# Attention over the input itself in a deep local-attention layer, with value and output weights multiplied beforehand, and expert mixing by gating the input

## The chip, the cores and the metric

The kernel runs on one core of one Trainium2 chip. The metric is the time of one execution on the device in microseconds (us), median over several runs. TensorE (PE) multiplies, VectorE (DVE), ScalarE (ACT) and GpSimd (POOL) work on elements, and SyncE (SP) starts the DMAs. Each engine takes its own instructions strictly in the order in which they are written; between engines there are counting semaphores and nothing else.

## The reference, cut to what matters

Twelve residual sublayers run over x of 4 units x 512 positions x 128 features, all in float32. The change touches three of their parts. The deep sublayer (called twice) is by far the longest:

```
for i in range(6):                                # DEPTH
    s = shift_tokens(x)
    q, k, v = split(s @ Wqkv[i])                  # 16 heads of 64
    q, k = l2norm(q) * qs, l2norm(k) * ks; rotary(q), rotary(k)
    attn = softmax(8 * q @ k2.T, masked)          # windows of 32 queries over 64 keys
    x = (attn @ v2) @ Wo[i] + x
    x = layernorm(shift_tokens(x)) -> gated gelu (341 hidden) -> + x
```

The mixture (called twice) is `gate = softmax(x @ Wg + bg)`, the top 2 of 8 experts kept and normalised, and `out = sum over e of gate[e] * (x @ We[e].T + be[e])`. Ahead of each of the twelve sublayers stands a plain layer norm.

## The kernel before, in words

Activations lie features by positions: 128 features on the partitions, 512 positions of a unit along the free axis. Four units (b = 0 to 3) go through each sublayer.

**Deep stage.** A call has 6 layers x 4 units = 24 units (`UNITS`) of 4 tiles of 128 positions, so 96 tiles. The order is written out by hand as a software pipeline: one step s handles tile s in its projection, tile s-1 in its norm and rotation's end, tile s-2 in its scores and softmax, and tile s-3 in the product of probabilities and values. n = s // 4 is the unit, t = s % 4 the place in it. Each engine has a loop over s (`deep_pe`, `deep_act`, `deep_dve`, `deep_pool`) that names its pieces in a fixed order, with extra pieces of the unit's end (output projection, layer norm, gated gelu) at particular t. On PE a step of the kernel before is:

1. `qk_pe(s, 0)`, L1307: queries, 2 matmuls of 512 columns. Here the step begins (called T0 below).
2. `scores_open_pe`, L1262 and L1276; `value_pe`, L1332 (4 matmuls of 64 x 512, two heads' halves in different columns of the array); `scores_close_pe`, L1276.
3. the unit's pieces of this t (t=0 variance, t=1 gate 0, t=2 hidden 2, t=3 rest of Wo).
4. `turn_pe(s-1, 0)`, L1320: 8 transposes of the rotated queries. It waits for POOL's `rope_scale_pool(s-1, 0)`, L1739, which waits for ACT's square root `norms_act(s-1)`, L1487. On ACT that stands behind `square_act(s, 0)`, L1480, which waits for piece 1.
5. `qk_pe(s, 1)` for the keys; `mix_open_pe(s-3)`, L1359 (probabilities x values, 32 small matmuls of 64 x 64 x 32 columns); `turn_pe(s-1, 1)`; `mix_close_pe`; `probs_turn_pe(s-2)`, L1290; and among them further pieces of the unit's end.

PE computes a float32 matmul as two passes, so 2 matmuls of 512 columns are 4 entries in the trace; a transpose (`is_transpose=True`) is one. The values of a window lie once in each half of the partitions; `value_act` evacuates half of them and four DMAs of SP (`move_values`) copy the rest.

**Mixture.** For each of 16 tiles of 128 positions PE forms all 8 experts' outputs (L375, 2 matmuls of 512 columns), DVE multiplies them by the gates (L473, 1024 elements) and adds over experts (L478), PE transposes the sum back (L400), and after four tiles DVE adds it to x (L463). One unit has four tiles.

**Layer norm ahead of a sublayer.** `quad_spread_pe`, L184, spreads 1/std over the partitions: 16 matmuls with the identity for four units, in two passes each; DVE's L206 scales with it.

Of the kernel before, what the change touches and what calls it, by code (L numbers as in the profile page):

```python
# [39 lines left out]
ODD_LAYER = 34430  # L40
# [5 lines left out]
def program(nc, d, out, sublayers):  # L46
    with ExitStack() as ctx:
# [19 lines left out]
        layered = [n for n in d if n.startswith("deep_")]  # L67
# [35 lines left out]

        kept = {n: sb("w_" + n, list(d[n].shape), d[n].dtype) for n in lasting}
# [72 lines left out]
        def quad_spread_pe(pe, q, b):  # L177
# [18 lines left out]
        def quad_centre_dve(dve, q, at_=small):  # L196
            for b in range(NB):
                dve.wait_ge(qn.qn_mean_ready, NB * q + b + 1)
                nc.vector.tensor_tensor(at_.xc[:, b, :], x[:, unit(b)], norm_bank(b), ALU.subtract).then_inc(qn.qn_centred, 1)
            dve.wait_ge(qn.qn_std_ready, q + 1)  # L200
            nc.vector.reciprocal(all_rstd[:, :], all_std[:, :]).then_inc(qn.qn_rstd_ready, 1)
# [125 lines left out]
        def swiglu_dve(dve, u, q, k):  # L327
# [3 lines left out]
            for b in range(NB):  # L331
# [5 lines left out]
                if b >= 1:  # L337
# [4 lines left out]
        mo = sems("moe_logits_ready moe_step moe_shifted moe_exped moe_gsum moe_ginv moe_gates_ready moe_gates_turned moe_gates_kept "  # L342
                  "moe_experts_ready moe_weighted moe_summed moe_out_ready")
# [26 lines left out]
        def moe_experts_pe(pe, k, i):  # L370
            b, t, a = i // TILES, i % TILES, 2 * (i % 2)
            if i >= 2:
                pe.wait_ge(mo.moe_weighted, TILES * k + i - 1)
            for h in range(2):
                last = nc.tensor.matmul(bank(a + h), qn_xn[:, b, 1 + t * P:1 + (t + 1) * P], w.moe_we[:, 4 * h:4 * h + 4, :],  # L375
                                        start=True, stop=True)
            last.then_inc(mo.moe_experts_ready, 1)

        def moe_gates_pe(pe, k, b):
# [5 lines left out]
            for t in range(TILES):  # L385
                last = nc.tensor.matmul(norm_bank(b)[0:EXPERTS, t * P:(t + 1) * P], gates[:, TILES * b + t, :], w.ident[:, :],
                                        start=True, stop=True)
            last.then_inc(mo.moe_gates_turned, 1)

        def moe_bias_pe(pe, u, k, b):  # L390
            if b >= 1:
                pe.wait_ge(g.unit_done, u + b)
            pe.wait_ge(mo.moe_gates_kept, k + b + 1)
            nc.tensor.matmul(bank(4), w.moe_be[:, :], gatesT[0:EXPERTS, b, :], start=True, stop=False, skip_group_check=True)

        def moe_turn_pe(pe, k, i):

            t = i % TILES
            pe.wait_ge(mo.moe_summed, TILES * k + i + 1)
            last = nc.tensor.matmul(bank(4)[:, t * P:(t + 1) * P], moe_acc[:, i % 2, :], w.ident[:, :],  # L400
                                    start=False, stop=(t == TILES - 1), skip_group_check=True)
            last.then_inc(mo.moe_out_ready, 1)

        def moe_pe(pe, u, q, k):
# [17 lines left out]
        def moe_act(act, q, k):
# [3 lines left out]
            for b in range(NB):  # L426
                act.wait_ge(mo.moe_gates_turned, k + b + 1)
                nc.scalar.activation(gatesT[0:EXPERTS, b, :], norm_bank(b)[0:EXPERTS, :], ACT.Copy).then_inc(mo.moe_gates_kept, 1)

        def moe_route_dve(dve, r):  # L430
# [27 lines left out]
            nc.vector.tensor_tensor(gates, ex, over(ginv, G), ALU.mult).then_inc(mo.moe_gates_ready, 1)  # L458
            dve.wait_ge(mo.moe_gates_ready, r + 1)

        def moe_out_dve(dve, k, b):
            dve.wait_ge(mo.moe_out_ready, TILES * (k + b + 1))
            nc.vector.scalar_tensor_tensor(x[:, unit(b)], bank(4), 0.5, x[:, unit(b)], ALU.mult, ALU.add).then_inc(g.unit_done, 1)  # L463

        def moe_dve(dve, u, q, k):
            quad_centre_dve(dve, q)
# [3 lines left out]
            for i in range(ROWS):  # L470
                a, n = 2 * (i % 2), TILES * k + i
                dve.wait_ge(mo.moe_experts_ready, n + 1)
                nc.vector.tensor_tensor(moe_prod[i % 2], psum[:, a * 512:(a + 2) * 512].rearrange("p (e o) -> p e o", o=P),  # L473
                                        over(gates[:, i, :], [P, EXPERTS, P]), ALU.mult).then_inc(mo.moe_weighted, 1)
                dve.wait_ge(mo.moe_weighted, n + 1)
                if i >= 2:
                    dve.wait_ge(mo.moe_out_ready, n - 1)
                nc.vector.tensor_reduce(moe_acc[:, i % 2, :], moe_prod[i % 2].rearrange("p e o -> p o e"), AX.X,  # L478
# [1618 lines left out]
```

## Time and profile before

| | us |
|---|---|
| median of 3 runs | 4492.48 (4480.17 to 4496.16) |
| profiled execution, its own time | 4489.61 |
| its span | 4487.9 |
| deep calls, about 1060 to 2720 and 2820 to 4488 of the span | some 3300 |
| mixtures, 11 to 94.4 and 373 to 456 | some 165 |

One execution was profiled. A matmul's end in the trace is modelled, so the time from the start of one group of matmuls to the start of the next is what PE spent on it. "128*64" in a row is the part of the array used (rows*columns), 128x512 the output. Idle time in square brackets names who ended it.

### The profile page before, as it was taken

What the parts mean: (1) busy time and instruction counts of PE and PEld (TensorE: products, weight loads), DVE (VectorE), ACT (ScalarE), POOL (GpSimd) and SP (SyncE); (2) the same over time, 40 slices, a digit from 0 to 9 for tenths busy, and PEclk for the clock granted to TensorE, in tenths of its full rate; (3) what the DMA queues carried; (4) which work ended last, traced back from release to release, by engine and by line L of the source; (5) the groups of instructions that cost most, each with busy time, mean ns of one, the idle gap of its engine ahead of it and who ended that gap; (6) DMA issues with size and microseconds to landing.
All of it is one profiled execution on the core that took longest, in us unless ns stands there. A gap on an engine that the chain in (4) does not pass through costs nothing.

```text
span 4487.9 us, 148433 instructions
## 1 busy us (share of the span) xinstructions
PE 4237.0 (94%) x66604; PEld 2403.9 (54%) x66604; DVE 3256.5 (73%) x4169; ACT 2676.0 (60%) x3161; POOL 2128.2 (47%) x1151
## 2 busy tenths in 40 slices
PE   7998899867999999999999996799999999999998
PEld 4544433434555555555555553455555555555554
DVE  6566666565877877877877866677877877877874
ACT  1451355323776776776776762466766766766764
POOL 0110000013665665666665650566666666666663
PEclk8998899978999999999999997899999999999999
DMA  2000000001111211121121111111211211121111
GB/s 84 1 2 1 0 1 1 1 0 35 33 33 29 58 33 54 33 58 30 33 58 29 33 33 50 24 31 31 58 32 31 58 32 55 33 57 30 33 33 29
DMA packets 78612, 144.88 MB, mean 32 GB/s; under 512 B 18648, under 2 KB 24992, under 8 KB 76448
## 3 DMA queue, kind: packets, MB, share of 16 engines
q1 hardware_dynamic: 77984, 135.39, 11.7%
q8 instruction: 530, 8.68, 0.8%
q14 instruction: 98, 0.80, 0.1%
HBM read 39.91 MB, written 1.05 MB: 9 GB/s over the span
## 4 chain that ended last, share of the span: by engine, by line
PE 77%; POOL 8%; issue 7%; DVE 6%; ACT 2%; DMA 0%; SPq 0%; POOLq 0%; DVEq 0%; ACTq 0%
PE psum L1307 13%; PE psum L1359 7%; PE psum L1332 6%; PE psum L1320 6%; PE psum L1276 5%; PE psum L667 5%; PE psum L1378 5%; PE psum L1290 4%; POOL arena L1739 3%; PE psum L1408 3%; PE psum L1424 3%; PE psum L1418 3%; PE psum L1373 3%; PE psum L699 3%; PE psum L721 3%
## 5 line engine op out<-in xcount | busy, mean ns | idle before, releaser
L1739 POOL TENSOR_TENSOR arena<-arena 128x1024 f32<-128x1024 f32 x384 | 722.3, 1902 | 881.8 <-ACT arena L1487 881.8
L1733 POOL TENSOR_TENSOR arena<-arena 128x1024 f32<-128x1024 f32 x384 | 907.5, 2363 | 245.0 <-DVE arena L1608 245.0
L1604 DVE TENSOR_TENSOR arena<-psum,arena 128x1024 f32<-128x1024 f32 x384 | 467.6, 1218 | 616.8 <-ACT arena L1480 616.6
L1480 ACT ACTIVATE arena<-psum 128x1024 f32<-128x1024 f32 x384 | 392.4, 1022 | 288.2 <-PE psum L1307 288.2
L1359 PEld LDWEIGHTS psum<-arena 64*64 64x64 f32 x24576 | 395.6, 135 | 211.8 <-issue 211.8
L1493 ACT ACTIVATE arena<-psum 128x1024 f32<-128x1024 f32 x384 | 390.8, 1018 | 194.6 <-PE psum L1320 194.6
L1608 DVE TENSOR_TENSOR arena<-psum,arena 128x1024 f32<-128x1024 f32 x384 | 466.4, 1215 | 0.0
L1615 DVE TENSOR_REDUCE h_pair<-arena 128x16 f32<-128x1024 f32 x384 | 464.2, 1209 | 0.0
L1359 PE MATMUL psum<-arena 64*64 64x32 f32 x24576 | 437.9, 221 | 5.2 <-DVE arena L1582 5.1
L1320 PE MATMUL psum<-w_ident,arena 128*128 128x128 f32 x3072 | 416.3, 279 | 23.5 <-POOL arena L1739 15.1
L1320 PEld LDWEIGHTS psum<-w_ident,arena 128*128 128x128 f32 x3072 | 338.2, 141 | 162.0 <-POOL arena L1739 94.6
L1307 PE MATMUL psum<-deep_wqkv,arena 128*128 128x512 f32 x768 | 378.6, 617 | 26.3 <-DVE arena L1608 19.3
L1745 POOL TENSOR_TENSOR arena<-arena 128x1024 f32<-128x1024 f32 x192 | 365.3, 1903 | 66.9 <-DVE arena L1592 58.4
L1276 PEld LDWEIGHTS psum<-arena 64*32 64x32 f32 x24576 | 292.9, 105 | 167.9 <-issue 157.8
L1307 PE MATMUL psum<-arena 128*128 128x512 f32 x768 | 361.9, 592 | 0.0
L1504 ACT ACTIVATE arena<-psum 128x1024 f32<-128x1024 f32 x192 | 196.7, 1024 | 257.9 <-PE psum L1290 251.6
L1276 PE MATMUL psum<-arena 64*32 64x64 f32 x24576 | 327.2, 223 | 0.3 <-issue 0.2
L667 PE MATMUL psum<-arena 32*128 32x512 f32 (+3 forms) x1024 | 303.6, 590 | 3.4 <-ACT arena L806 2.3
L1497 ACT ACTIVATE arena<-arena 128x1024 f32<-128x1024 f32 x192 | 202.9, 1057 | 173.8 <-DVE arena L1582 173.8
L699 PE MATMUL psum<-arena 32*128 32x512 f32 (+3 forms) x1024 | 293.3, 558 | 1.8 <-ACT arena L831 1.8
L1575 DVE TENSOR_REDUCE arena<-psum 128x16 f32<-128x1024 f32 x192 | 235.2, 1225 | 61.1 <-PE psum L1276 61.1
L831 ACT ACTIVATE arena<-psum 128x512 f32<-128x512 f32 (+3 forms) x344 | 161.0, 514 | 170.8 <-PE psum L699 169.4
(266 smaller groups left out, 7087.0 us busy)
## 6 DMA issues: line engine op xcount, KB each, us to landing
arena<-arena SPq DMA_DIRECT2D x672, 128.0 KB, 2.4
deep_wqkv<-in_deep_wqkv SPq DMA_DIRECT2D x6, 1536.0 KB, 7.2
arena<-in_deep_wqkv SPq DMA_DIRECT2D x6, 1536.0 KB, 7.1
arena<-arena SPq DMA_DIRECT2D x96, 64.0 KB, 2.0
deep_wo<-in_deep_wo SPq DMA_DIRECT2D x6, 512.0 KB, 7.5
arena<-in_deep_wo SPq DMA_DIRECT2D x6, 512.0 KB, 7.5
deep_w<-in_deep_w SPq DMA_DIRECT2D x6, 341.0 KB, 7.6
arena<-in_deep_w SPq DMA_DIRECT2D x6, 341.0 KB, 7.6
```

What stands on the lines that cost most here:

```text
L667: nc.tensor.matmul(bank(v % SCORE_BANKS)[:, 0:keys], da_Q[r32, b * SETS + s, x_ * P:(x_ + 1) * P], keys_of(causal, b, s)[r32, 0:keys], sta ...
L699: nc.tensor.matmul(bank(key_at[m])[:, q0:T], kk[r32, kt * P:(kt + 1) * P], da_Q[r32, b * SETS + s, q0:T], start=True, stop=True).then_inc( ...
L1276: last = nc.tensor.matmul(bank(r)[32 * jj:32 * jj + 32, pair * 64:pair * 64 + 64], qT[j % 2][r64, pair, jj * WIN:(jj + 1) * WIN], kT[r64, ...
L1307: last = nc.tensor.matmul(bank(2 + cc), xs[unit_ % 2][:, WIN + t * P:WIN + (t + 1) * P], wqkv[:, half * INNER + cc * 512:half * INNER + (c ...
L1320: last = nc.tensor.matmul(turns[:, m * P:(m + 1) * P], roped[a % 2][:, h:h + 2, :], w.ident[:, :], start=True, stop=True, is_transpose=True)
L1359: last = nc.tensor.matmul(bank(odd)[64 * side:64 * side + 64, to:to + WIN], V[64 * r:64 * r + 64, WPT * t + jj, (pair + odd) * 64:(pair + ...
L1480: nc.scalar.activation(qk_sq[:, HALVES[half], :], qk_half, ACT.Square).then_inc(de.deep_qk_squared, 1)
L1604: nc.vector.tensor_tensor(turned[:, hs, :].rearrange("p h (a e) -> p h a e", a=2), swapped, sin, ALU.mult).then_inc(de.deep_rope_parts, 1)
L1608: nc.vector.tensor_tensor(roped[a % 2][:, hs, :], qk_half, under(tabs[:, 2 * half, t, :], shape), ALU.mult).then_inc(de.deep_rope_parts, 1)
L1615: nc.vector.tensor_reduce(h_pair[:, hs, 0], qk_sq[:, hs, :], AX.X, ALU.add).then_inc(de.deep_sq_summed, 1)
L1733: nc.gpsimd.tensor_tensor(roped[a % 2][:, hs, :], roped[a % 2][:, hs, :], turned[:, hs, :], ALU.add).then_inc(de.deep_summed, 1)
L1739: nc.gpsimd.tensor_tensor(roped[a % 2][:, hs, :], roped[a % 2][:, hs, :], over(h_inv[a % 2][:, hs], [P, LHEADS, LD]), ALU.mult).then_inc(d ...
```

## The change

**Deep attention.** Instead of values V = X Wv and then P V Wo, the kernel forms P X (probabilities of a head times the input of the 64 keys, 128 features wide), and multiplies that by Wv_h Wo_h, a 128 x 128 matrix for each of the 16 heads.

- `value_pe` and `value_act` go. `xt_pe` (2 transposes) and `xt_act` (256 elements) put the transposed input of the tile's windows into `XA`; two DMAs (`move_keys`) make `XB`, the same with halves exchanged.
- `mix_pe` has 4 matmuls of 64 x 128 x 256 columns in each of its two parts instead of 32 of 64 x 64 x 32. Each part now fills both banks 0 and 1, so part 1 waits until ACT's `o_act(part 0)` has emptied them; ACT copies 1024 elements per part (`Y`), twice a tile instead of once.
- `out_pe` replaces `wo_first_pe` and `wo_rest_pe`: per unit 2 halves x 16 heads of 256 columns instead of 8 matmuls of 512 columns.
- `fold_pe` computes Wv_h Wo_h: 4 matmuls of 128 columns a unit for 20 of the 24 units (the next layer's), and 16 ahead of each call, between the layer norm's statistics and its spread. `fold_act` copies them.
- The unit's end moves by one tile or more: mean at the end of t=0, variance at t=1, gate 0, 1 and 2 at t=2, a 0 and 1 at t=3, a 2 and down at t=0 of the following unit. Gate, gelu and a use bank 7 alone, so gate 1 waits for gelu 0 and gate 2 for gelu 1.

**Mixture.** `moe_spread_pe` spreads the gates of four experts over the partitions (4 matmuls of 32 x 128 x 512 columns side by side), DVE multiplies the input by them (4 x 512 elements), and `moe_expert_pe` adds up 8 matmuls of 512 columns and one of the bias per unit in PSUM. Two rounds of four experts a unit, 8 rounds in all.

**Layer norm.** `quad_spread_pe` gets `is_transpose=True`: one pass instead of two.

```diff
-        def value_pe(pe, c, a):
...
-            for q in range(2):
-                wi = WPT * t + 2 * q + 1
                 for r in range(2):
-                    last = nc.tensor.matmul(turns[64 * r:64 * r + 64, q * 512:(q + 1) * 512],
-                                            xs[unit_ % 2][:, WIN * wi:WIN * wi + 2 * WIN], vw[:, r, :, :], start=True, stop=True)
+        def xt_pe(pe, c, a):
...
+            for n in range(2):
+                at = WIN * (WPT * t + n)
+                last = nc.tensor.matmul(turns[:, n * P:(n + 1) * P], xs[unit_ % 2][:, at:at + P], w.ident[:, :], start=True, stop=True,
+                                        is_transpose=True)
+        def mix_pe(pe, c, j, part):
+            if part == 0:
...
+            else:
+                pe.wait_ge(de.deep_o_kept, 2 * i + 1)
+            for side in range(2):
+                for r in range(2):
+                    r64, jj = slice(64 * r, 64 * r + 64), 2 * part + side
+                    keys = (XA if r == part else XB)[j % 2]
+                    last = nc.tensor.matmul(bank(r)[:, side * 256:(side + 1) * 256], keys[r64, side, :], weights[r64, :, jj, :],
+                                            start=True, stop=True)
+        def fold_pe(pe, c, layer, k, to):
+            for n in range(FOLD_HEADS):
+                pair, r64 = FOLD_HEADS * (k // 2) + n, slice(64 * (k % 2), 64 * (k % 2) + 64)
+                last = nc.tensor.matmul(to[:, n * P:(n + 1) * P], unfolded["deep_wvt"][r64, pair, :], unfolded["deep_wo"][r64, pair, :],
+                                        start=True, stop=True)
+        def out_pe(pe, c, m, half, part):
...
+            for h in range(8 * part, 8 * part + 8):
+                at = (h % 2) * 256 + (h // 2) * WIN
+                last = nc.tensor.matmul(bank(6)[:, half * 256:half * 256 + 256], vo[:, h, :], Y[half][:, :, at:at + WIN],
+                                        start=(h == 0), stop=(h == LHEADS - 1))
         def gate_pe(pe, c, m, j):
...
-                pe.wait_ge(de.deep_gelu_done, 3 * g_ + 1)
+                pe.wait_ge(de.deep_gelu_done, 3 * g_ + j)
+                if t == 1 and 1 <= n <= FOLDED_UNITS:
+                    fold_next_pe(pe, c, n)
+                if t == 0 and ending:
+                    out_pe(pe, c, n - 2, 1, 1)
+                if t >= 1 and begun:
+                    out_pe(pe, c, n - 1, (t - 1) // 2, (t - 1) % 2)
                 if 0 <= s - 3 < ALL:
-                    mix_close_pe(pe, c, s - 3)
+                    mix_pe(pe, c, s - 3, 1)
```

On PE, a step of a full unit with t=2 in the kernel before, from T0 on (L1307 projection, L1332 values, L1418 hidden 2, L1320 the turn of queries and then keys, L1359 mix, L1424 down, L1373 Wo):

```order
L1307 MATMUL psum<-deep_wqkv,arena 128x512 x2
L1262 MATMUL psum<-maskb,identb 32x512 x8
L1276 MATMUL psum<-arena 32x64 x32
L1332 MATMUL psum<-deep_wqkv,arena 64x512 x4
L1276 MATMUL psum<-arena 32x64 x32
L1418 MATMUL psum<-xc,deep_w_0 85x512
L1320 MATMUL psum<-w_ident,arena 128x128 x8
L1307 MATMUL psum<-deep_wqkv,arena 128x512 x2
L1359 MATMUL psum<-arena 64x32 x32
```

The same step in the changed kernel (L1326 projection, L1349 `xt_pe`, L1438 gate, L1339 turn, L1368 mix, L1403 `out_pe`):

```order
L1326 MATMUL psum<-arena 128x512 x2
L1279 MATMUL psum<-maskb,identb 32x512 x8
L1293 MATMUL psum<-arena 32x64 x32
L1349 MATMUL psum<-w_ident,arena 128x128 x2
L1293 MATMUL psum<-arena 32x64 x32
L1438 MATMUL psum<-xc,deep_w_0 128x512
L1339 MATMUL psum<-w_ident,arena 128x128 x8
L1326 MATMUL psum<-arena 128x512 x2
L1368 MATMUL psum<-arena 128x256 x4
L1339 MATMUL psum<-w_ident,arena 128x128 x8
L1438 MATMUL psum<-xc,deep_w_0 128x512
L1403 MATMUL psum<-arena 128x256 x8
```

The values' four matmuls stood ahead of the first turn and are two transposes now; `out_pe` stands behind the second turn (at t=1, 2 and 3), and a second gate stands between that turn and `out_pe`.

ACT in the changed kernel in the same step, from behind the square of the queries (L1520 root of the norms, L1570 affine, L1553 `xt_act`, L1530 exp, L1526 turn copy, L1513 square, L1575 gelu, L1545 `o_act`):

```order
L1520 ACT_TABLE_LOAD
L1520 ACTIVATE arena<-arena 128x32
L1570 ACTIVATE xc<-xc,deep_vec 128x512
L1553 ACTIVATE arena<-psum 128x256
L1530 ACT_TABLE_LOAD
L1530 ACTIVATE arena<-arena 128x1024
L1526 ACTIVATE arena<-psum 128x1024
L1513 ACTIVATE arena<-psum 128x1024
L1575 ACT_TABLE_LOAD
L1575 ACTIVATE arena<-psum,deep_vec 128x512
L1545 ACTIVATE arena<-psum 128x1024
L1526 ACTIVATE arena<-psum 128x8x128
```

The root stands where it stood, behind the first square of its step, and the first gelu stands behind the exp, one copy and the second square, as in the kernel before (there at t=1).

## Rows read from the trace of the kernel before

**Rows 1.** The page, busy time of each engine in the whole span.
```profile
PE 4237.0 (94%) x66604; PEld 2403.9 (54%) x66604; DVE 3256.5 (73%) x4169; ACT 2676.0 (60%) x3161; POOL 2128.2 (47%) x1151
```
**Rows 2.** One full unit: length, busy time of engines, granted clock, DMA share.
```profile
1779.42:1846.62 67.20, 66.93 (x1266) 39.61 (x1265) 52.71 (x60) 47.41 (x51) 44.13 (x25) 1.00 0.14 32
```
**Rows 3.** Timeline of PE, step t=2: start, length, engine, line, operation.
```profile
1822.48 1.88 PE L1307 MATMUL psum<-deep_wqkv,arena 128*128 128x512 f32 x4
1824.29 0.41 PE L1262 MATMUL psum<-maskb,identb 64*32 64x512 bf16 x8
...
1825.29 1.94 PE L1332 MATMUL psum<-deep_wqkv,arena 128*64 128x512 f32 x8
1827.15 0.86 PE L1276 MATMUL psum<-arena 64*32 64x64 f32 x64
1827.94 1.09 PE L1418 MATMUL psum<-xc,deep_w 128*85 128x512 f32 x2
1829.06 1.09 PE L1320 MATMUL psum<-w_ident,arena 128*128 128x128 f32 x8
1829.99 1.88 PE L1307 MATMUL psum<-deep_wqkv,arena 128*128 128x512 f32 x4
1831.80 1.14 PE L1359 MATMUL psum<-arena 64*64 64x32 f32 x64
1832.87 1.09 PE L1320 MATMUL psum<-w_ident,arena 128*128 128x128 f32 x8
...
1834.95 2.85 PE L1424 MATMUL psum<-arena,deep_w 128*128 128x512 f32 x6
1837.64 2.74 PE L1373 MATMUL psum<-arena,deep_wo 128*128 128x512 f32 x6
1840.21 1.04 PE L1290 MATMUL psum<-w_ident,arena 128*128 128x128 f32 x8
1841.09 1.88 PE L1307 MATMUL psum<-deep_wqkv,arena 128*128 128x512 f32 x4
```
**Rows 4.** Timeline of PE, where the steps t=0 and t=1 begin.
```profile
1791.38 1.88 PE L1307 MATMUL psum<-deep_wqkv,arena 128*128 128x512 f32 x4
...
1805.58 1.88 PE L1307 MATMUL psum<-deep_wqkv,arena 128*128 128x512 f32 x4
```
**Rows 5.** Timeline of ACT and POOL, same step t=2 from its first square.
```profile
1824.39 1.02 ACT L1480 ACTIVATE arena<-psum 128x1024 f32<-128x1024 f32 x1 [1.55 <-PE psum L1307]
...
1825.44 1.28 ACT L1487 ACT_TABLE_LOAD   x1
...
1826.73 0.23 ACT L1487 ACTIVATE arena<-arena 128x32 f32<-128x32 f32 x1
...
1827.10 3.76 POOL L1739 TENSOR_TENSOR arena<-arena 128x1024 f32<-128x1024 f32 x2 [5.13 <-ACT arena L1487]
...
1830.57 1.06 ACT L1497 ACTIVATE arena<-arena 128x1024 f32<-128x1024 f32 x1 [0.97 <-DVE arena L1582]
```
**Rows 6.** Timeline of ACT, step t=1: the first two gelus.
```profile
1817.86 1.27 ACT L1536 ACTIVATE arena<-psum,deep_vec 128x512 f32<-128x512 f32 x2
```
**Rows 7.** Timeline of PE: matmuls in two row halves of the array, elsewhere.
```profile
114.45 1.99 PE L590 MATMUL psum<-arena 64*128 64x512 f32 x8
...
116.28 1.02 PE L594 MATMUL psum<-arena 64*128 64x512 f32 x2
```
**Rows 8.** Timeline of PE, a layer norm: variances and spread.
```profile
102.80 3.63 PE L173 MATMUL psum<-w_avg,arena 128*128 128x1 f32 x32
...
107.08 5.46 PE L184 MATMUL psum<-w_ident,all_rstd 128*128 128x128 f32 x32 [0.65 <-DVE all_rstd L201]
```
**Rows 9.** Timeline of DVE: last scaling behind that spread.
```profile
112.66 0.69 DVE L206 TENSOR_TENSOR z<-arena,psum 128x512 f32<-128x512 f32 x1 [0.20 <-PE psum L184]
```
**Rows 10.** Timeline of DVE: gates ready, last sum of the first mixture.
```profile
36.95 0.29 DVE L458 TENSOR_TENSOR arena<-arena 128x128 f32<-128x128 f32 x1
...
93.69 0.69 DVE L463 SCALAR_TENSOR_TENSOR x<-psum,x 128x512 f32<-128x512 f32 x1 [0.58 <-PE psum L400]
```

More of the change, by code:

```diff
@@ L66, in program @@
         maskb = sb("maskb", [P, 2, 2 * WIN], BF16)
-        layered = [n for n in d if n.startswith("deep_")]
+        folded = ["deep_wo", "deep_wvt"]
+        layered = [n for n in d if n.startswith("deep_") and n not in folded]
         x = sb("x", [P, NB * T])
@@ L469, in moe_dve @@
             moe_route_dve(dve, k // NB)
[L470 to L478, printed above, removed]
-                                        ALU.add).then_inc(mo.moe_summed, 1)
-                if i % TILES == 0 and i:
-                    moe_out_dve(dve, k, i // TILES - 1)
+            for n in range(ROUNDS * NB):
+                b, h = n // ROUNDS, n % ROUNDS
+                for l in range(LANES):
+                    i = LANES * (ROUNDS * k + n) + l
+                    if l == 0:
+                        dve.wait_ge(mo.moe_gate_spread, ROUNDS * k + n + 1)
+                    if n >= 1:
+                        dve.wait_ge(mo.moe_used, i - LANES + 1)
+                    nc.vector.tensor_tensor(moe_in[:, l, :], bank(l), now(b), ALU.mult).then_inc(mo.moe_weighted, 1)
+                if h == 0 and b >= 1:
+                    moe_out_dve(dve, k, b - 1)
             moe_out_dve(dve, k, NB - 1)
@@ L1213, in program @@
         kT = new(PAIRS, WIN + T)
-        V = new(T // WIN, T)
+        XA, XB = ([new(2, P) for _ in range(2)] for _ in range(2))
+        Y = [new(2 * WPT, LHEADS * WIN) for _ in range(2)]
+        VO = [new(LHEADS, P) for _ in range(2)]
+        FOLDS, FOLD_HEADS = 4, LHEADS // 4
         qk_sq = new(2 * LHEADS, LD)
@@ L1219, in program @@
         probsT = new(2, T)
-        oT = new(PAIRS, T)
         hidden = new(3, T)
@@ L1388, in var_pe @@
-        def var_pe(pe, c, m):
-            pe.wait_ge(de.deep_squared, c * UNITS + m + 1)
+            if n <= FOLDED_UNITS:
+                pe.wait_ge(de.deep_fold_kept, folds(c, n))
+            pe.wait_ge(de.deep_squared, g_ + 1)
             for t in range(TILES):
-                last = nc.tensor.matmul(bank(6)[:, t:t + 1], xc_sq[:, t * P:(t + 1) * P], w.avg[:, 0:1], start=True, stop=True)
+                last = nc.tensor.matmul(bank(7)[:, t:t + 1], xc_sq[:, t * P:(t + 1) * P], w.avg[:, 0:1], start=True, stop=True)
@@ L1468, in deep_pe @@
                 if t == 0 and ending:
+                    mean_pe(pe, c, n - 2)
+                if t == 1 and ending:
                     spread_pe(pe, c, n - 2)
-                if t == 1 and ending:
-                    a_pe(pe, c, n - 2, 1)
         def square_act(act, c, a, half):
@@ new lines, in o_act, with xt_act @@
+            first = WPT * (t % 2) + 2 * part
+            nc.scalar.activation(Y[t // 2][:, first:first + 2, :].rearrange("p w (r e) -> p w r e", r=2),
+                                 psum[:, 0:1024].rearrange("p (r w e) -> p w r e", r=2, w=2), ACT.Copy).then_inc(de.deep_o_kept, 1)
+        def xt_act(act, c, a):
+            i = c * ALL + a
+            act.wait_ge(de.deep_xt_ready, i + 1)
+            if a >= 2:
+                act.wait_ge(de.deep_pv_done, 2 * (i - 1))
+            nc.scalar.activation(XA[a % 2], turns[:, 0:2 * P].rearrange("p (w f) -> p w f", f=P), ACT.Copy).then_inc(de.deep_xt_kept, 1)
@@ L1522, in ln_square_act, with fold_act @@
+        def fold_act(act, c, layer, k, src):
+            act.wait_ge(de.deep_fold_ready, FOLDS * (c * DEPTH + layer) + k + 1)
+            pairs = slice(FOLD_HEADS * (k // 2), FOLD_HEADS * (k // 2 + 1))
+            nc.scalar.activation(VO[layer % 2].rearrange("p (a r) f -> p r a f", r=2)[:, k % 2, pairs, :],
+                                 src.rearrange("p (a f) -> p a f", f=P), ACT.Copy).then_inc(de.deep_fold_kept, 1)
         def ln_square_act(act, c, m):
@@ L1535, in gelu_act @@
             act.wait_ge(de.deep_gate_ready, 3 * (c * UNITS + m) + j + 1)
-            nc.scalar.activation(hidden[0:rows, j, :], bank(6 + j % 2)[0:rows, :], ACT.Gelu,
+            nc.scalar.activation(hidden[0:rows, j, :], bank(7)[0:rows, :], ACT.Gelu,
                                  bias=layer_of(m).vec[0:rows, 6 + j:7 + j]).then_inc(de.deep_gelu_done, 1)
@@ L1909, in _ @@
                     quad_stats_pe(pe, u, q)
+                    for k in range(FOLDS):
+                        fold_pe(pe, call, 0, k, bank(k))
                     for b in range(NB):
@@ L1940, in _ @@
                     quad_act(act, q)
+                    for k in range(FOLDS):
+                        fold_act(act, call, 0, k, bank(k))
                     deep_act(act, call)
```

361 lines of the change are left out of this document (180 added, 181 removed).

## The prediction

> **What bounds the kernel now.** I read the page's busy times first, then single units of the deep stage, then the timeline of one step. The page has PE busy in 94% of the span and no other engine over 73% [rows 1]. In a full unit of the deep stage PE is busy for 66.93 of 67.20 us at granted clock 1.00, that is 2.4 GHz, while DVE has 52.7, ACT 47.4 and POOL 44.1 [rows 2]. So PE's queue is the clock of that stage, and the reader should look at how it fills a step. The busy figure hides one thing, and the timeline shows it. In the step t=2 the first turn starts 1829.06 - 1822.48 = 6.58 us behind the step's start T0 [rows 3]. The group ahead of it, two passes of 512 columns, has 1.12 us, although such a pass takes 0.427 to 0.43 us (1.81 for four, 2.69 for six, 2.57 for six). The turn is held, and the other engines' rows say by what: the square of the queries starts at T0 + 1.91 (behind the projection's 1.81), a table load at 2.96, the root at 4.25, and POOL's two scalings from 4.62 on, 1.88 each, the first ending at 6.50 [rows 5]. This chain root -> POOL -> turn has a length of 6.58 us whatever PE does meanwhile. Today PE has just enough in front of the turn: 1.81 + 1.00 (mask and scores) + 1.86 (values) + 0.79 (scores) + some 0.95 for two passes = 6.4.
>
> **The change part by part.** First PE's work alone, per full unit, from starts to starts.
>
> Values: 1.86 us a tile [rows 3] become two transposes. Eight transposes have 0.93 or 0.88 us, so 0.107 each; two and the change of the array's tiling 0.15 make 0.37. 4 x (0.37 - 1.86) = -6.0.
>
> Mix: a half has 1.07 now [rows 3]. The new half is four matmuls of 64 rows x 128 columns, eight passes of 256 columns, 0.214 each (half of 0.427). The nearest rows are eight passes of 512 columns in the two row halves: 116.28 - 114.45 = 1.83 us, so two passes at a time, 4 x 0.43 and 0.11 [rows 7]. For 256 columns that is 4 x 0.214 + 0.15 = 1.01. Bounds: 0.85 with nothing around it, 1.87 if the halves went one behind the other. I take 1.01, from the row of the same form. 8 x (1.01 - 1.07) = -0.5.
>
> Output: 2 halves x 16 heads x 2 passes = 64 passes of 0.214 = 13.7, for 16 passes of 0.428 = 6.85. +6.8. A pass needs its own weights. The 32 variance passes, of one column with 128 x 128 weights each, have 3.63 / 32 = 0.113 us [rows 8], so a load takes at most that, and the 512-column passes hide theirs. Bounds: hidden (0.214) or not (0.327, +7.2 a unit). I take hidden.
>
> Fold: 8 passes with a weight load each, 8 x 0.113 + 0.2 = 1.1, in 20 of 24 units: +0.9. Its bank waits for the unit's end, which DVE reaches at the end of step t=0, before PE asks.
>
> Work alone: -6.0 - 0.5 + 6.8 + 0.9 = +1.3 us per unit. But what goes is ahead of the turn, and what comes is mostly behind it, so I redo the steps with the chain. Before, their lengths are 14.20 (t=0), 16.90 (t=1), 18.61 (t=2) [rows 3, 4], and 67.20 - 49.71 = 17.49 (t=3).
>
> - t=3. Ahead of the turn stand 1.81 + 1.00 + 0.37 + 0.79 + 0.95 = 4.9; the turn still starts at 6.58, so 1.7 us are waited. Then turn 0.93, keys 1.81, mix 1.01, turn 0.93, output half 3.52 (16 passes and a change of tiling), mix 1.01, hidden 1 0.93, transposes of the probabilities 0.88: 17.6.
> - t=2. Again 6.58, then 0.93 + 1.81 + 1.01 + 0.93 to 11.3. Gate 1 then waits for the first gelu, since both now use bank 7. ACT reaches it as at t=1 today, where the two gelus start at 1817.86, 12.28 us behind that T0, so the first ends at 12.9 [rows 4, 6]; the exp, which leads that queue, starts at 8.1 in this step as well [rows 5]. So gate 1 starts at 12.95, 1.6 late. Then 0.86 + 3.52 + 1.01 + 0.93 + 0.88: 20.15. Queued behind gate 1 are output half, mix and the next step, so the whole queue shifts.
> - t=1. `fold_act` (some 0.6, half of a 1.02 copy and its overhead) stands ahead of the root, so the turn starts at 7.2; then 0.93 + 1.81 + 1.01 + 0.93 + 3.52 + 1.01 + 0.88 + 0.43: 17.7.
> - t=0. Hidden 2 and an output half precede the turn: 1.81 + 1.00 + 0.37 + 0.79 + 0.95 + 3.42 = 8.34, so the chain is covered. Then 0.93 + 1.81 + 1.01 + 0.93, down 2.69, 1.01, 0.88, mean 0.86: 18.45.
>
> Sum 73.9, +6.7, and 6.6 with the four units that fold nothing. A call has 22 full units: +146. In unit n=1, which has no layer norm yet, three output halves (10.5) replace the first six passes of Wo (2.6) and the last ten, of which 3.3 lie beyond the chain: +4.6. Two calls: +301.
>
> ACT gets a second copy a tile (1.02) for the value copy that goes, and the exchange of halves has a whole step for its two DMAs instead of four: both lie beside PE. The wait of mix part 1 for the copy of part 0 is covered by the turn and output half between them (4.4 us); without these it would cost about 1.
>
> Each call gains 16 folds ahead of the spread, 32 x 0.113 = 3.6 us in a gap of 0.65 [rows 8]: +6 for both. Its end has one step more, a chain of waits without projections: +5 each by estimate (bounds 0 and 10): +10.
>
> Mixture: from gates to the end of the last sum the first one takes 94.38 - 37.24 = 57.1 us [rows 10], bound by DVE. The new one is bound by PE: 8 rounds of 8 passes of 0.43 (3.42) plus a spread (two passes deep, 0.86, and 0.25 for the changes of tiling) = 4.55; 36.4, three biases 2.6, and some 5.5 until the first product: 44.5. -12 each, bounds -8 and -15: -24.
>
> Spread: 107.08 to 113.35, 6.27 us [rows 8, 9]. With one pass DVE's four scalings bound it, 4 x 0.69 + 0.8: 3.6, -2.6. Of twelve, about six look like this one; the others have DVE or ACT work of their sublayer between, and I give them 1 or less. -20, bounds -8 and -31.
>
> Profiled time 4489.61 + 301 + 6 + 10 - 24 - 20 = 4763; the median of the runs is 2.9 higher, so 4765.
>
> A rule that speaks against this change: the Trainium skill, "TensorE: Matmul & The Clock Gate", section on the mechanism of row and column tiling, says that a weight load runs beside matmuls in flight only where its row group differs; elsewhere the page also has a background weight buffer. By the strict rule output passes, all of 128 rows, would pay their load each. The trace does not agree: full-height passes of 512 columns follow each other at 0.427 with loads between them.
>
> **The rivals.**
>
> 1. *No added wait; only work.* The first turn comes as soon as PE is there. For it: the turn waits for only some 0.2 us today. Against: the 6.58 us are measured from T0 and contain nothing that goes. Unit +1.3 less the waits of today (0.5): 4489.6 + 44 x 0.8 + 9 + 16 - 44 = 4506, or 4528 with these waits kept. I name 4517.
> 2. *Mix halves one behind the other*, 1.87: +0.86 x 7 (one of eight hides ahead of gate 1), 6.0 a unit, +270: 5030. Against it rows 7. *Weight loads not hidden* under 256 columns gives +7.2 a unit in its place, 5080.
> 3. *The clock falls* where PE waits 1.6 us three times a unit. If 5 us of a unit's passes ran at 1.2 GHz instead of 2.4, that adds 5: +220, 4985. Against: the waits are short against the 16 us around them.
> 4. *Faster.* Place: the root's start on ACT. If ACT, freed of the value copy, and POOL have the queries scaled before PE arrives, the turn starts at T0 + 5.0; it decides as soon as that start is under 5.5. With mix at its bound of 0.85 (-1.7), the unit has -6.0 - 1.7 + 6.8 + 0.9 - 0.5 = -0.5, and with the outer gains at -15 and -25: 4489.6 - 22 + 16 - 55 = 4430. For it: V's work is the one large group at 1.86 that goes. Against: the square that precedes the root waits for this step's projection, not for the value copy.
>
> **How the numbers follow.** Forecast 0.74, rival 1 0.06, rival 2 0.07 (both forms), rival 3 0.06, rival 4 0.07. The predicted time is 4765. Its own spread, from the bounds of copies, ends and outer stages, is about 4690 to 4850. Eight in ten: I cut rival 4 and 1 below and most of rival 2 above, and reach 4600 to 5000. A run of this kernel tells 0.5%, some 22 us, from no change. Faster 0.07; within it 0.03 (half of rival 1); slower 0.90.
>
> **What would show it.** In the changed profile a full unit lasts near 74 us at clock 1.00. PE's busy share falls to about 90%. L1339 waits for POOL's scaling at t=1, 2 and 3, starting 6.6 to 7.2 behind T0, and L1438 waits 1.6 us for ACT's gelu. Two L1368 groups have 1.0 us, L1403 3.4 to 3.5. Gates to last sum take 44 us. Wrong would be a unit of 68 (rival 1), an L1368 group of 1.9, an L1403 group of 5 or a granted clock below 0.95 in full units; the forecast falls if the first turn starts earlier than 6.4 behind T0.

## The result and the profile after

| | us |
|---|---|
| changed kernel, median of 4 runs | 4879.68 (4858.39 to 4881.87) |
| kernel before, median beside them | 4489.19 (4480.17 to 4496.16) |
| ratio | 1.0853, 95% interval 1.0821 to 1.0885 |
| profiled execution after, span | 4880.2 (before 4487.9) |

The change makes the kernel 8.5% slower: +390 us, where +276 was forecast. The page's busy line of the changed kernel answers to [rows 1]:

```profile
PE 4405.7 (90%) x46476; PEld 2701.7 (55%) x46476; DVE 3182.9 (65%) x4171; ACT 2765.7 (57%) x3401; POOL 2123.9 (44%) x1149
```

Two full units of the changed deep stage, one behind the other; columns as in [rows 2] (length, busy time of PE, PEld, DVE, ACT and POOL, granted clock, DMA share):

```profile
1632.72:1708.56 75.84, 70.64 (x851) 46.72 (x849) 52.29 (x61) 49.35 (x55) 42.27 (x21) 0.98 0.08 22
1708.56:1782.90 74.34, 69.14 (x850) 45.60 (x849) 52.30 (x61) 49.24 (x55) 42.23 (x21) 1.00 0.04 9
```

At full clock a unit takes 74.34 us where it took 67.20, of which PE is busy 69.14 instead of 66.93. So 2.2 us of the 7.1 are more work; 4.9 are PE standing still. The first of the two units has 1.5 us more, at a granted clock of 0.98. It holds a few half-clock passes at t=1 (granted clock 0.91 in that step). Now PE's timeline (start, length, operation, what ended the idle time before), changed kernel, for t=2 and then t=3, which answers to [rows 3]:

```profile
1745.07 1.88 PE L1326 MATMUL psum<-deep_wqk,arena 128*128 128x512 f32 x4
...
1750.31 1.12 PE L1438 MATMUL psum<-xc,arena 128*128 128x512 f32 x2 [1.20 <-ACT xc L1570]
1751.65 1.09 PE L1339 MATMUL psum<-w_ident,arena 128*128 128x128 f32 x8 [0.21 <-POOL arena L1783]
1752.58 1.88 PE L1326 MATMUL psum<-deep_wqk,arena 128*128 128x512 f32 x4
1754.39 1.13 PE L1368 MATMUL psum<-arena 64*128 64x256 f32 x8
1755.46 1.09 PE L1339 MATMUL psum<-w_ident,arena 128*128 128x128 f32 x8
1757.76 1.13 PE L1438 MATMUL psum<-xc,arena 128*128 128x512 f32 x2 [1.21 <-ACT arena L1575]
1758.72 3.62 PE L1403 MATMUL psum<-arena 128*128 128x256 f32 x16
1762.27 1.13 PE L1368 MATMUL psum<-arena 64*128 64x256 f32 x8
...
1765.13 1.88 PE L1326 MATMUL psum<-deep_wqk,arena 128*128 128x512 f32 x4
...
1769.10 1.12 PE L1448 MATMUL psum<-xc,arena 128*128 128x512 f32 x2
1771.72 1.09 PE L1339 MATMUL psum<-w_ident,arena 128*128 128x128 f32 x8 [1.49 <-POOL arena L1783]
```

In both steps the first turn (L1339) starts 6.58 to 6.59 us behind T0. At t=2 this is to the hundredth what it was in the kernel before, although the values ahead of it are 1.5 us shorter; most of that time stands ahead of gate 0, which waits for ACT's affine. At t=3 the turn waits 1.49 for POOL, and there the kernel before looks different:

```profile
1846.55 4.56 PE L1378 MATMUL psum<-arena,deep_wo 128*128 128x512 f32 x10
1850.95 1.04 PE L1320 MATMUL psum<-w_ident,arena 128*128 128x128 f32 x8
```

Its step t=3 begins at 1841.09, so its first turn starts 9.86 behind T0 and waits for nothing: ten passes of the output product stand ahead of it and cover the chain. The changed kernel has its output piece behind the second turn, and so the chain is uncovered at t=3 as well. Gate 1 (the second L1438) starts at T0 + 12.69 and waits 1.21 for the gelu. A mix part takes 1.07, an output piece 3.55.

### The profile page after: what moved, and what is told of

Its sections match the earlier page's. It is cut to its first block, busy times and chain, and to the rows that moved or that the text cites. A ratio compares the mean times of both kernels' runs of the same rounds, so it can differ in the third digit from the quotient of the medians.

```text
span 4880.2 us, 108445 instructions
## 1 busy us (share of the span) xinstructions
PE 4405.7 (90%) x46476; PEld 2701.7 (55%) x46476; DVE 3182.9 (65%) x4171; ACT 2765.7 (57%) x3401; POOL 2123.9 (44%) x1149
## 4 chain that ended last, share of the span: by engine, by line
PE 71%; ACT 9%; issue 8%; DVE 7%; POOL 4%; DMA 0%; POOLq 0%; SPq 0%; ACTq 0%; DVEq 0%
PE psum L1403 13%; PE psum L1326 13%; PE psum L1368 7%; PE psum L1339 6%; PE psum L683 4%; POOL arena L1783 4%; PE psum L1307 4%; PE psum L715 3%; PE psum L737 3%; ACT L1520 2%; PE psum L1454 2%; ACT arena L1513 2%; PE psum L1438 2%; PE psum L1448 2%; PE psum L1293 1%
## 5 line engine op out<-in xcount | busy, mean ns | idle before, releaser
L1545 ACT ACTIVATE arena<-psum 128x1024 f32<-128x1024 f32 x384 | 393.9, 1026 | 622.2 <-PE psum L1368 617.6
L1403 PE MATMUL psum<-arena 128*128 128x256 f32 x3072 | 699.3, 381 | 0.0
L1403 PEld LDWEIGHTS psum<-arena 128*128 128x128 f32 x3072 | 579.0, 191 | 118.7 <-issue 47.9
L1513 ACT ACTIVATE arena<-psum 128x1024 f32<-128x1024 f32 x384 | 392.5, 1022 | 321.2 <-PE psum L1326 321.2
L1339 PE MATMUL psum<-w_ident,arena 128*128 128x128 f32 x3072 | 441.4, 289 | 129.2 <-POOL arena L1783 125.1
L1339 PEld LDWEIGHTS psum<-w_ident,arena 128*128 128x128 f32 x3072 | 352.6, 146 | 280.9 <-POOL arena L1783 206.7
L1368 PE MATMUL psum<-arena 64*128 64x256 f32 x3072 | 438.2, 404 | 5.0 <-DVE arena L1626 3.8
L1526 ACT ACTIVATE arena<-psum 128x1024 f32<-128x1024 f32 x384 | 390.9, 1018 | 45.8 <-PE psum L1339 45.8
L1326 PE MATMUL psum<-deep_wqk,arena 128*128 128x512 f32 x768 | 390.2, 633 | 25.6 <-DVE arena L1652 19.3
L1368 PEld LDWEIGHTS psum<-arena 64*128 64x128 f32 x3072 | 266.5, 187 | 248.5 <-issue 231.4
L1326 PE MATMUL psum<-arena 128*128 128x512 f32 x768 | 372.1, 608 | 0.0
L1530 ACT ACTIVATE arena<-arena 128x1024 f32<-128x1024 f32 x192 | 203.4, 1059 | 250.2 <-DVE arena L1626 250.2
L683 PE MATMUL psum<-arena 32*128 32x512 f32 (+3 forms) x1024 | 309.7, 603 | 3.4 <-ACT arena L822 2.3
L715 PE MATMUL psum<-arena 32*128 32x512 f32 (+3 forms) x1024 | 305.4, 587 | 1.8 <-ACT arena L847 1.8
```

Source lines behind the costliest of these rows:

```text
L683: nc.tensor.matmul(bank(v % SCORE_BANKS)[:, 0:keys], da_Q[r32, b * SETS + s, x_ * P:(x_ + 1) * P], keys_of(causal, b, s)[r32, 0:keys], sta ...
L1326: last = nc.tensor.matmul(bank(2 + cc), xs[unit_ % 2][:, WIN + t * P:WIN + (t + 1) * P], wqk[:, half * INNER + cc * 512:half * INNER + (cc ...
L1339: last = nc.tensor.matmul(turns[:, m * P:(m + 1) * P], roped[a % 2][:, h:h + 2, :], w.ident[:, :], start=True, stop=True, is_transpose=True)
L1368: last = nc.tensor.matmul(bank(r)[:, side * 256:(side + 1) * 256], keys[r64, side, :], weights[r64, :, jj, :], start=True, stop=True)
L1403: last = nc.tensor.matmul(bank(6)[:, half * 256:half * 256 + 256], vo[:, h, :], Y[half][:, :, at:at + WIN], start=(h == 0), stop=(h == LHE ...
L1513: nc.scalar.activation(qk_sq[:, HALVES[half], :], qk_half, ACT.Square).then_inc(de.deep_qk_squared, 1)
```

## The experiments

Times are medians; the ratios are to runs of the kernel before made beside them on the same chip (medians 4490.54 to 4494.57 us).

**1. Output piece ahead of the first turn.**

```diff
+                if t >= 1 and begun:
+                    out_pe(pe, c, n - 1, (t - 1) // 2, (t - 1) % 2)
                 if 0 <= s - 1 < ALL:
                     turn_pe(pe, c, s - 1, 0)
...
-                if t >= 1 and begun:
-                    out_pe(pe, c, n - 1, (t - 1) // 2, (t - 1) % 2)
```

> The changed kernel with the output product's pieces of t=1, 2 and 3 moved on PE from behind the second turn to ahead of the first turn; nothing else. Theory (the first turn cannot start before T0 + 6.6 whatever PE does, so work behind it adds and work ahead of it is free up to there): the step t=3 falls from 17.8 to 16.1-16.4, t=2 from 20.1 to 17.3-17.6 (gate 1 then comes after the first gelu by itself), t=1 from 18.0/19.5 to 17.5; a unit from 75.1 to 69.5, 22 units in two calls: 245 us less than the changed kernel, about 4635. Mix part 1 may wait 0.2-0.5 for the copy of part 0, since only one turn is left between them. Rival (the stage is bound by PE's work, and the added work is what it costs): same work, same time, 4880.

Measured: 4735.1, ratio 1.0535 (1.0507 to 1.0564). So 145 us of the changed kernel's 390 come back, 100 less than expected. PE's timeline of t=3 in this kernel:

```profile
1730.14 1.88 PE L1326 MATMUL psum<-deep_wqk,arena 128*128 128x512 f32 x4
...
1735.07 3.62 PE L1403 MATMUL psum<-arena 128*128 128x256 f32 x16
1738.52 1.04 PE L1339 MATMUL psum<-w_ident,arena 128*128 128x128 f32 x8
...
1743.56 1.13 PE L1368 MATMUL psum<-arena 64*128 64x256 f32 x8 [0.20 <-ACT arena L1545]
```

The turn waits for nothing now, at 8.38 behind T0, and t=3 falls from 17.77 to 16.32. But mix part 1 follows at once on the second turn and waits for ACT's copy of part 0 (L1545): 0.20, and 0.36 from starts to starts, as the expectation allowed. The missing 100 us lie at t=2, where hardly anything is won: 19.74 measured (20.06 before the edit) and 17.3 to 17.6 expected, some 2.3 in each of 44 units. PE waits three times for ACT there. Gate 0, which still stands ahead of the output piece, waits 1.21 for the affine; in the changed kernel the same wait lay within the hold of the turn and cost next to nothing. Gate 1's wait (1.03) moves along: its gelu stands on ACT behind the second square, and that behind the keys' projection, which the output piece has pushed back. Gate 2 waits 0.22 for the second gelu.

**2. POOL's first scaling for one head of 16.** The queries of 15 heads stay unscaled.

```diff
+            h0 = slice(LHEADS * half, LHEADS * half + 1)
...
+            else:
+                nc.gpsimd.tensor_tensor(roped[a % 2][:, h0, :], roped[a % 2][:, h0, :], over(h_inv[a % 2][:, h0], [P, 1, LD]),
+                                        ALU.mult).then_inc(de.deep_roped, 1)
```

> The changed kernel with POOL's scaling of the queries done for one head in 16 only (the part left out: 15 of 16 heads of the queries are not scaled by their norm), 1.9 us to some 0.1 in each step. If the chain root, scaling, turn were the only hold, the first turn would start when PE is there, T0 + 4.9 to 5.2 in t=3, and t=1 and 3 would fall by 1.5 each, some 130 us in all: 4750. Theory as I now read the trace: there is a second chain of almost the same length, squares, DVE's rotation, maximum, subtraction, exp and copy of the turned queries, at the end of which the second turn waits, at T0 + 10.1, while it starts at 10.4 now. So t=3 and t=1 fall by 0.3 to 0.5 each, t=2 (held by gate 1) by nothing: 35 us less, 4845, with new waits of the second turn for ACT's copy.

Measured: 4764.3, 1.0613 (1.0592 to 1.0634). The total lies near the 4750 expected for a single chain, and the trace says the opposite. t=3 fell by 0.55 only, of 1.6 waited (17.77 to 17.22), t=1 by 0.57, t=2 by nothing. PE at t=3 of this kernel:

```profile
1721.32 1.09 PE L1339 MATMUL psum<-w_ident,arena 128*128 128x128 f32 x8
1722.25 1.88 PE L1326 MATMUL psum<-deep_wqk,arena 128*128 128x512 f32 x4
1724.33 1.13 PE L1368 MATMUL psum<-arena 64*128 64x256 f32 x8 [0.19 <-DVE arena L1626]
1726.22 1.06 PE L1339 MATMUL psum<-w_ident,arena 128*128 128x128 f32 x8 [0.76 <-ACT arena L1526]
```

The first turn goes at 4.97 behind T0, and the second then waits for ACT's copy of the first (L1526), which stands on ACT behind the exp, and the exp behind DVE's softmax (L1626). So there is a second chain, and it has only 0.5 us of slack: it lets the second turn go at 9.87 behind T0, where it went at 10.39. The steps give 44 x 1.12 = 49 us. The other 77 of the 126 between the profiled spans have other sources: no t=1 in the middle of a call has half clock any more (about 35 us in all), the unchanged attention stage took 276.4 instead of 295.9 (below), and the rest is spread over the calls' edges and small stages. The total alone would have given the wrong verdict.

**3. Gate 1 behind the output piece at t=2.**

```diff
-                if t == 2 and ending:
-                    gate_pe(pe, c, n - 2, 1)
                 if t >= 1 and begun:
                     out_pe(pe, c, n - 1, (t - 1) // 2, (t - 1) % 2)
+                if t == 2 and ending:
+                    gate_pe(pe, c, n - 2, 1)
```

> The changed kernel with gate 1 of step t=2 moved behind the output piece of that step, so that it comes 14.8 us behind T0, after the first gelu has freed bank 7 at 12.9. Theory: its wait of 1.2 to 1.4 us goes and nothing takes its place; t=2 falls from 20.07 to 18.65, 44 units: 62 us less, 4818. Rival: ACT is late with everything in this step and gate 2 or the mix waits as long: 4880.

Measured: 4814.4, 1.0715 (1.0698 to 1.0732), as expected: t=2 falls from 20.06 to 18.59, and the others stay where they run at full clock. The gelu is ready while the output runs.

**4. Both in one:** the output first at t=1 and t=3, gate 1 late at t=2.

```diff
+                if t in (1, 3) and begun:
+                    out_pe(pe, c, n - 1, (t - 1) // 2, (t - 1) % 2)
                 if 0 <= s - 1 < ALL:
                     turn_pe(pe, c, s - 1, 0)
...
+                if t == 2 and begun:
+                    out_pe(pe, c, n - 1, 0, 1)
                 if t == 2 and ending:
                     gate_pe(pe, c, n - 2, 1)
-                if t >= 1 and begun:
-                    out_pe(pe, c, n - 1, (t - 1) // 2, (t - 1) % 2)
```

> The output piece stands ahead of the first turn at t=1 and t=3 (as in the run with the output first) and at t=2 it stays behind the second turn, with gate 1 behind it (as in the run with the late gate). If what the two edits saved adds up, the steps are 18.56, 17.70, 18.59 and 16.32, together 71.2 against 74.3 to 75.9 now, and the whole is 4735 less 44 x (19.74 - 18.59) = 4685. If the time won at t=1 and t=3 comes back as a wait in the step behind (a turn held by POOL at t=2, an exp that comes later), t=2 has some 19.4 and the whole 4720. Even at 4685 the deep calls stay 3.9 us a unit over those of the kernel before, since the work of the output and the folds stays.

Measured: 4694.89, 1.0442 (1.0414 to 1.047). A full unit, and its steps t=0 to t=3:

```profile
1652.05:1723.22 71.17, 68.67 (x851) 45.93 (x849) 52.12 (x62) 49.86 (x55) 42.29 (x22) 1.00 0.04 9
1652.05:1670.60 18.55, 18.55 (x214) 11.76 (x213) 14.99 (x19) 11.94 (x13) 11.05 (x6) 1.00 0.03 8
1670.60:1688.30 17.70, 16.82 (x223) 12.39 (x222) 11.58 (x13) 11.98 (x15) 10.10 (x6) 1.00 0.04 10
1688.30:1706.90 18.60, 17.18 (x211) 10.91 (x210) 13.64 (x17) 14.64 (x17) 11.48 (x6) 1.00 0.04 9
1706.90:1723.22 16.32, 16.12 (x209) 10.86 (x207) 11.90 (x14) 11.30 (x13) 9.65 (x5) 1.00 0.04 10
```

The savings add up. Of the 185 us gained, 167 lie between the first and last projections of the two calls (85.7 and 81.7): that much of the 390 hangs on the order on PE. The shorter steps make 44 x 3.17 = 139 of it; most of the rest is that fewer units have half clock at t=1. A unit still has 71.17 against 67.20: 1.7 more work than before and 2.5 idle (0.3 before).

**5. The freed work put back as dummies:** each tile's two input transposes done eight times.

```diff
-            for n in range(2):
+            for n in 8 * (0, 1):
```

> Changed kernel, with the two input transposes of each tile done eight times over (14 extra passes, 14 x 0.107 = 1.5 us a tile, as much as the values' matmuls took more): output unchanged. If every step is held by chains that count from T0, t=3 and t=2 take it for nothing (1.65 us waited there each), t=1 takes 1.3 of it, t=0 none: +1.7 a unit, less the clock's falls at t=1 (0.75 a unit): 4925. If the later scores also delay DVE's softmax and the exp, and with it the copy that the second turn needs, t=1 to t=3 grow by another 0.8 each: 5030. If PE were simply full, every tile pays: +6 a unit, 5145.

Measured: 4915.84, 1.0936 (1.091 to 1.0963), 9 us under the first of the expected times. At full clock the steps are 20.08, 18.20, 20.43 and 17.77 against 18.56, 17.95, 20.06 and 17.77. Of 6.1 us more work a unit only 2.1 show, in t=0 alone in full. At t=3 of this kernel:

```profile
1750.80 1.88 PE L1326 MATMUL psum<-deep_wqk,arena 128*128 128x512 f32 x4
...
1753.61 1.97 PE L1349 MATMUL psum<-w_ident,arena 128*128 128x128 f32 x16
...
1757.39 1.09 PE L1339 MATMUL psum<-w_ident,arena 128*128 128x128 f32 x8
```

1.5 us of dummies and still a turn at 6.59 behind T0. So with this order on PE, taking the values' matmuls away buys nothing at t=3 and little at t=1 and t=2. The second chain did not reach the second turn here: at t=2 and t=3 the second turn starts 10.39 behind T0, as it does without the dummies.

**6. The last unit of a call spread over banks.** With the serial bank 7, the three gate blocks and the three a blocks of a call's last unit wait for each other though nothing else is left to run.

```diff
+        def ffn_bank(m, i):
+            return bank((7, 2, 3, 4, 5, 0)[i] if m == UNITS - 1 else 7)
...
-            if j == 0:
+            if j == 0 or m == UNITS - 1:
```

> Changed kernel; only in the last unit of each call gates 1, 2 and the three a blocks go to banks 2, 3, 4, 5 and 0, which are free by then, instead of bank 7, so none waits for the gelu or hidden block before it. If the serial use of bank 7 makes half of the longer end of a call, the stretch from gate 0 of the last unit to the next stage falls from 24.07 us to the 12.8 of the kernel before, the part from the last projection to the next stage from 105.6 to 94.3, and the whole by 2 x 11.3 to 4857. If that stretch is long because its passes run at half clock (6 passes of 512 columns take 5.2 us there), it falls by 3 or less a call: 4875.

Measured: 4848.38, 1.0779 (1.074 to 1.0818), span 4854.6. PE from gate 0 of the last unit of call 0 to the next stage (L170): first the kernel before, then the changed one, then this one.

```profile
2719.24 4.55 PE L1408 MATMUL psum<-xc,arena 128*128 128x512 f32 x6 [1.62 <-ACT xc L1531]
2723.70 3.13 PE L1418 MATMUL psum<-xc,arena 128*128 128x512 f32 x6
2727.74 2.84 PE L1424 MATMUL psum<-arena 128*128 128x512 f32 x6 [0.91 <-DVE arena L1663]
2732.02 1.13 PE L168 MATMUL psum<-x,w_avg 128*128 128x512 f32 x2 [1.44 <-DVE x L1981]
```

```profile
2898.87 2.08 PE L1438 MATMUL psum<-xc,arena 128*128 128x512 f32 x2 [1.63 <-ACT xc L1570]
2901.72 2.08 PE L1438 MATMUL psum<-xc,arena 128*128 128x512 f32 x2 [0.78 <-ACT arena L1575]
...
2907.35 2.07 PE L1448 MATMUL psum<-xc,arena 128*128 128x512 f32 x2 [0.77 <-ACT arena L1575]
2910.34 2.07 PE L1448 MATMUL psum<-xc,arena 128*128 128x512 f32 x2 [0.91 <-DVE arena L1707]
...
2916.24 5.26 PE L1454 MATMUL psum<-arena 128*128 128x512 f32 x6 [0.91 <-DVE arena L1707]
2922.94 1.13 PE L170 MATMUL psum<-x,w_avg 128*128 128x512 f32 x2 [1.44 <-DVE x L2030]
```

```profile
2891.10 5.38 PE L1441 MATMUL psum<-xc,arena 128*128 128x512 f32 x6 [1.63 <-ACT xc L1575]
2896.31 2.74 PE L1453 MATMUL psum<-xc,arena 128*128 128x512 f32 x6
2899.96 2.84 PE L1459 MATMUL psum<-arena 128*128 128x512 f32 x6 [0.91 <-DVE arena L1712]
2904.24 1.13 PE L170 MATMUL psum<-x,w_avg 128*128 128x512 f32 x2 [1.44 <-DVE x L2035]
```

12.78, 24.07 and 13.14 us. From the last projection to the next stage the two calls take 10.8 and 10.9 us less than in the changed kernel; 22 of the 31 between the medians were expected. The five added waits of 0.77 to 0.91 are only part of it, 4.2: in the changed kernel two passes of an a last 2.07 and down's six 5.26, in this one six passes last 2.74 and 2.84. Between the short waits the changed kernel works at half clock (1.2 GHz): the granted clock is 0.54 over these 24.07 us. This one is back at 2.4 GHz behind the gates (1.00 from 2896.3 to 2904.2).

**7. The outer parts alone** (mixture and spread; deep stage as before).

```diff
+                                        w.ident[:, :], start=True, stop=True, is_transpose=True)
...
+        def moe_spread_pe(pe, k, n):
...
+        def moe_expert_pe(pe, k, n, l):
...
```

> The kernel before with the mixture by gated input and the one-pass spread of the layer norms, and its deep stage as before. Theory from the two traces: each mixture gains 11 us, the spreads 1 to 2.5 each, 15 in all, so 37 less if the clock falls nowhere else: 4452. Rival: the unchanged attention sublayer behind the first mixture, which took 20 us more in the changed kernel at a granted clock of 0.88 in a stretch that had 1.00, loses its clock because of what now precedes it; then 17 less, 4472.

Measured: 4464.6, 0.9936 (0.9911 to 0.9962): 0.6% faster than the kernel before, though 12 us less so than expected; its attention stage had the long form (below). Each part by itself, first the spread (the first line of that diff), then the mixture (the rest):

> Kernel before with the one-pass spread alone. By its term in the prediction (-20) 4471; by the stages' lengths in the run with both outer parts (the stages other than mixture and attention lost 9 together) about 4478. If the attention stage's longer half-clock stretch comes with the spread, 17 more: 4488 to 4495.

Measured: 4485.85, 0.9982 (0.9971 to 0.9993), about -5.

> Kernel before with the new mixture alone. By its term in the prediction (-24) 4467, with the attention stage as long as before (276). If the half-clock stretch of the attention stage comes from how the mixture ahead of it ends, that stage has 292 and the whole is 4483; then some executions may fall to the shorter one, 17 us apart.

Measured: 4465.63, 0.9947 (0.9935 to 0.9959), -25. The mixture gives its 25 us. The spread does what was forecast on the spot: the twelve stretches from spread to last scaling lose 19.7 us together (0.5 to 3.1 each). But what follows in the same stages grew by 11.2 and the statistics by 2.0, and the mean granted clock went from 0.964 to 0.961. The attention stage is not the reason, it had its short form (274.5). Which of these stretches lost it to the clock was not taken apart.

**8. The deep part alone:** the changed kernel with spread and mixture of before.

```diff
-                                        w.ident[:, :], start=True, stop=True, is_transpose=True)
+                                        w.ident[:, :], start=True, stop=True)
...
-        def moe_spread_pe(pe, k, n):
...
-        def moe_expert_pe(pe, k, n, l):
...
```

> Only the deep part of the change (mixture and spread as before). The deep calls cost the same +199 each from stage to stage. The outer parts, which cost -35 us in the run with these alone once the half-clock stretch of the unchanged attention stage is taken off (-19 with it), are missing. So 4895 to 4905 if that stage's clock is as in the kernel before, 4915 if it is as in the changed one; 4880 if the outer parts are worth nothing beside the deep one.

Measured: 4907.28, 1.0921 (1.0899 to 1.0942). Of the two parts' effects, -27 and +413, the sum is +386, and both together measured +390. An interaction of more than some ten us is not seen.

**The stage that nobody changed.** The multi-query attention between the two mixtures has the same code in all these kernels. Whole stage, four traces (before, changed, outer parts alone, mixture alone), columns as above:

```profile
97.20:373.20 276.00, 264.48 (x2272) 134.47 (x2273) 165.60 (x552) 125.81 (x296) 40.60 (x64) 0.95 0.01 1
```

```profile
85.70:381.60 295.90, 285.28 (x2257) 139.68 (x2258) 165.75 (x552) 126.13 (x296) 40.60 (x64) 0.86 0.01 1
```

```profile
84.60:377.20 292.60, 281.93 (x2256) 137.96 (x2257) 165.73 (x552) 126.13 (x296) 40.61 (x64) 0.87 0.00 1
```

```profile
87.30:361.90 274.60, 262.97 (x2272) 133.78 (x2273) 165.79 (x552) 125.76 (x296) 40.60 (x64) 0.96 0.01 1
```

DVE's and ACT's busy times are equal to 0.4 us; PE's differ by up to 22, with the clock. Of the twelve traces five had the long form (changed, 1, 3, 6, 7) and seven the short one (before, 2, 4, 5, 8 and each outer part alone), 274 to 277 against 292.5 to 296. The four times of run 7 (4450.29, 4458.46, 4470.7, 4475.31) and the 4858.39 among the changed kernel's others near 4880 fit two such forms about 20 us apart. Experiments 2, 4 and 5 have the changed kernel's outer parts and the short form. What chooses between them stays open.

## Why the prediction was right, and where its sizes were off

- **The hold of the first turn, right.** It was the main step: 6.58 behind T0 whatever PE does. After: 6.58 at t=2, 6.59 at t=3, 7.24 at t=1 (7.2 forecast). Experiment 5 shows it from the PE's side, and experiment 2 from POOL's: with a short scaling the turn starts at 4.97. Rival 1 (only work) would have needed a unit near 68. One limit the prediction did not name: its reading of t=2 holds in the kernel before for t=0, 1 and 2, while at t=3 the turn started 9.86 behind T0, behind the output product. What t=3 lost is the cover of that work.
- **The lengths of the steps, right** to 0.3: 18.56, 17.95, 20.06, 17.77 against 18.45, 17.7, 20.15, 17.6. Together 0.44 more than forecast, times 44 units 19 us, less 6 because a call's first full unit has no down at t=0 (15.42). Gate 1 starts at 12.69 (12.95 forecast).
- **Prices of the groups.** Mix part 1.07 (1.01), transposes of the input 0.37 (0.37), output 3.45 to 3.55 (3.42 to 3.52), fold 1.08 (1.1). So rival 2 falls in both forms: the halves of the mix run side by side, and the loads of 256-column passes are hidden.
- **Half clock, mis-sized.** The prediction gave it a case of its own or nothing. It came small: 18.74 instead of 17.95 at t=1 on average. Of the 44 units 19 have 19.45 to 19.64, and the last three of each call, which fold nothing, 18.72 to 18.98 for the 17.30 they have at full clock (experiment 3). Together some 39 us. In experiment 5 no t=1 has it, in experiment 2 none in the middle of a call. Rival 3 (+220) was too big by far, but its place in the forecast, zero, was wrong too.
- **The ends of the calls, mis-sized.** From last projection to next stage 84.0 became 105.7, and 86.4 became 110.6: +45.9 against +10. Half of it is the step that the prediction left out: it worked out in full what bank 7 costs at t=2, 1.6 us, and did not carry this to the end of a call, where it costs 10.8 and 10.9 (experiment 6). The other half wasn't taken apart by a run; in it lie the extra step and the last unit's four output pieces, 14 us for 6.85.
- **The outer parts.** Mixture -25 by its own run (-24 forecast): right in the total. From gates to last sum the first one takes 47.2 in the changed kernel (35.62 to 82.79), where 44.5 were forecast and 57.1 stood before. Spread -5 (-20 forecast): on the spot the saving came (19.7), though in the run with the spread alone the stretch named has 4.26 instead of 3.6 and DVE still waits 0.47 and 0.17 for PE in it, so the four scalings alone did not bound it. What failed is the assumption that the stages end earlier by as much. Folds ahead of the spread +4.3 and +3.5 (+6).
- Summed against the profiled spans: first to last projection +175.7 a call, +351.4 (301 forecast; of the 50 above it about 39 are the clock and 13 the steps); ends +45.9; all the rest -5.0 (-38 forecast), in which the unchanged attention stage's long form has +19.9. Together 392.3. These 20 us come from a stage that the change doesn't touch. That they have nothing to do with the change isn't shown, since the kernel before was traced only once.
- The forecast was 276 and the rise 390. The prediction's own spread, 4690 to 4850, was too narrow; the measured 4880 lies in its wider range alone. The reason for the wait was right, and the sizes missed were the ends, the clock and the spread.

## What to carry to other kernels

Work that is removed ahead of a held instruction buys nothing; what is added behind it is paid in full, and the same work moved from ahead of it to behind it is paid as well (t=3). Before counting matmuls, find from which event each wait counts, put long pieces of work in front of it, and look for the second chain that ends just behind the first. When banks are merged, price the serial use also where nothing else is left to run, at the end of a stage.

## What the hardware showed that was not expected

- Row pairs of 64 rows x 128 columns with passes of 256 columns run two at a time: eight in 1.07 us; full-height passes of 256 columns follow each other at 0.22 (16 in 3.45 to 3.55), each with its own weights.
- One unchanged stage of PE work, DVE and ACT equal, took 274 to 277 or 292.5 to 296 us, in traces of kernels that differ elsewhere; where the clock was read, it was 0.95 and 0.96 or 0.86 and 0.87.
- More work can go with a better clock. At t=1, 25 of the changed kernel's 44 units hold a stretch at half clock, and experiments 6 and 8, whose full units have the same code, show nearly the same pattern; with 1.5 us of dummy transposes a tile no unit does.
